# Taking the constant 160 off again on VectorE instead of ScalarE, in a fused layer kernel on eight cores

## What is computed

```python
xn    = layernorm(x)                              # per token, no weights
B, C  = xn @ W2 + b2, xn @ W3 + b3                # 16 columns each
delta = softplus(xn @ W1 + b1)                    # 1024 columns
s     = xn * delta * sum(B * C, axis=-1)          # the einsums collapse to this
xh    = xn @ H                                    # Hadamard, 1024 x 1024, / 32
sc    = max(abs(xh)) / 7                          # per token
xq    = clip(round(xh / sc), -8, 7) * sc
wq    = ternary(weight)                           # -1, 0, 1 times a scale per output row
g     = silu(xq @ wq.T)
out   = x + s * g
```

## Time and profile before

| | us |
|---|---|
| median of 3 runs | 528.99 (528.32 to 529.50) |
| the profiled execution | 529.43 |
| its span on the slowest core, core 0 | 527.9 |
| spans of the eight cores | 523.0 to 527.9 |

### The profile page before, as it was taken

The page is one execution under the profiler, slowest core; times in us unless marked ns, Lnnn a source line. Parts: engine busy times, 40 slices in busy tenths (PEclk is TensorE's granted clock), DMA queues, the critical chain, the costliest instruction groups (busy, mean ns, idle before and its releaser), DMA issues.

```text
span 527.9 us, 7192 instructions; the slowest of 8 cores (523.0 to 527.9 us)
## 1 busy us (share of the span) xinstructions
PE 351.1 (67%) x1696; PEld 149.1 (28%) x1696; DVE 305.9 (58%) x600; ACT 344.0 (65%) x393; POOL 323.4 (61%) x215
## 2 busy tenths in 40 slices
PE   0023260997979697877978787787789779757200
PEld 0001220443424243332433333333333334322000
DVE  1418886455766666666667666667666654542210
ACT  1603143569796979888888888888888777654220
POOL 6000160112677777777777777777777777767763
PEclk9997575798979899997989899989988999896655
DMA  7992321243654454444445445444544334222110
GB/s 146 247 261 65 110 61 23 57 94 78 140 120 116 120 153 122 120 122 120 119 120 121 120 125 128 124 125 119 133 135 133 80 81 99 61 61 60 41 78 40
DMA packets 80973, 57.78 MB, mean 109 GB/s; under 512 B 70435, under 2 KB 70564, under 8 KB 80932
## 3 DMA queue, kind: packets, MB, share of 16 engines
q1 hardware_dynamic: 72916, 34.19, 29.9%
q0 software_dynamic: 8016, 23.14, 13.6%
HBM read 25.93 MB, written 16.78 MB: 81 GB/s over the span
## 4 chain that ended last, share of the span: by engine, by line
POOL 48%; DVE 17%; issue 12%; PE 9%; DMA 5%; ACT 4%; POOLq 1%; DVEq 1%; SPq 1%; ACTq 0%
POOL ob L33 13%; POOL t4b L33 13%; POOL t1b L33 11%; DVE t3b L33 7%; POOL uT L33 5%; POOL vT L33 5%; DMA xnT<-xnb 3%; DVE tbf L33 3%; DMA xb<-x 3%; DVE absum L33 2%; PE psZ L268 1%; PE psZ L269 1%; PE psO L289 1%; DVE cst L33 1%; PE psO L290 1%
## 5 line engine op out<-in xcount | busy, mean ns | idle before, releaser
L33 POOL TENSOR_TENSOR t4b<-t3b,o3s 128x1024 f32<-128x1024 f32 x32 | 75.2, 2351 | 69.4 <-DVE t3b L33 69.4
L289 PE MATMUL psO<-ternT,xqT 128*128 128x512 bf16 x256 | 100.6, 393 | 13.6 <-DMA xqT<-xqb 8.3
L268 PE MATMUL psZ<-W1c,xnT 128*128 128x512 bf16 x256 | 101.0, 395 | 0.5 <-DVE bcw L33 0.5
L269 PE MATMUL psZ<-W1c,xnT 128*128 128x512 bf16 x256 | 100.3, 392 | 0.0
L290 PE MATMUL psO<-ternT,xqT 128*128 128x512 bf16 x256 | 100.2, 391 | 0.0
L312 PE MATMUL psXH<-Hs,uT 128*128 128x512 bf16 x128 | 58.3, 456 | 45.2 <-ACT xqm L33 41.0
L33 DVE SCALAR_TENSOR_TENSOR t3b<-xnb,cc,t1b 128x1024 f32<-128x1024 bf16 x32 | 41.1, 1284 | 73.4 <-POOL t1b L33 73.0
L33 POOL TENSOR_TENSOR ob<-xb,t4b 128x1024 f32<-128x1024 f32 x32 | 75.4, 2355 | 4.6
L33 POOL TENSOR_TENSOR t1b<-del,s 128x1024 f32<-128x1024 bf16 x32 | 68.6, 2143 | 7.9 <-ACT s L33 4.1
L33 ACT ACTIVATE esb<-psO,nsa 128x1024 f32<-128x1024 f32 x32 | 35.7, 1114 | 52.1 <-DVE o3s L33 51.6
L33 POOL TENSOR_TENSOR uT<-xnT 128x512 bf16<-128x512 bf16 x32 | 37.2, 1164 | 38.3 <-DMA xnT<-xnb 37.4
(11 more groups left out here) (53 smaller groups left out, 509.3 us busy)
## 6 DMA issues: line engine op xcount, KB each, us to landing
xb<-x SPq DMA_DIRECT2D x32, 512.0 KB, 4.1
out<-ob POOLq DMA_DIRECT2D x32, 512.0 KB, 3.4
wfst<-wf POOLq DMA_DIRECT2D x8, 512.0 KB, 4.2
W1c<-w POOLq DMA_DIRECT2D x8, 256.0 KB, 17.6
Hs<-hpk SPq DMA_DIRECT2D x1, 512.0 KB
xnT<-xnb SPq DMA_TRANSPOSE x32, 3.0
xqT<-xqb SPq DMA_TRANSPOSE x32, 3.1
W23s<-w POOLq DMA_DIRECT2D x1, 64.0 KB, 3.5
```

The costliest lines, as they stand in the source:

```text
L33: inst = fn(*a, **kw)
L268: pe.matmul(psZ1[:, 0:512], lh, W1c[ic][:, 0:512], start=(ic == 0), stop=False)
L269: pe.matmul(psZ1[:, 512:1024], lh, W1c[ic][:, 512:1024], start=(ic == 0), stop=False)
L289: pe.matmul(ps[:, 0:512], lh, ternT[:, ic * DM:ic * DM + 512], start=(ic == 0), stop=(ic == KC - 1))
```

## The change

The instruction that makes `xqb` goes from ScalarE to VectorE. There it is a `tensor_single_scalar` with the immediate -160.0 and `ALU.add`, bfloat16 in and out, written between `dot` and `o3s`. The wait for the transpose of the tile before goes with it, and VectorE gets a wait on `sRND`, which ScalarE sets when `xqm` is done. The semaphore `sXQB` that SP waits for is now set by VectorE.

```diff
@@ scalar
                     ac.wait_ge(sMX, u + 1)
                     ac.activation(xqm[:], psXH[:], AF.Identity, scale=inv[u % 2][:],
                                   bias=c160s[:], _inc=(sRND, u + 1))
-                    if u >= 1:
-                        ac.wait_ge(sTXQa[(u - 1) % 2], 16 * ((u - 1) // 2 + 1))
-                    ac.activation(xqbf[:], xqm[:], AF.Identity, bias=nc160s[:], _inc=(sXQB, u + 1))
                 w_ = c - 3
@@ vector
                     dv.tensor_reduce(dot[td % 2][:], prod[:], AX.X, ALU.add)
+                uq = c - 1
+                if 0 <= uq < nt:
+                    dv.wait_ge(sRND, uq + 1)
+                    if uq >= 1:
+                        dv.wait_ge(sTXQa[(uq - 1) % 2], 16 * ((uq - 1) // 2 + 1))
+                    dv.tensor_single_scalar(xqbf[:], xqm[:], -160.0, ALU.add, _inc=(sXQB, uq + 1))
 
                 w_ = c - 3
```

## The result

| | before | after |
|---|---|---|
| median of 8 runs, us | 529.10 (528.32 to 529.76) | 567.02 (566.31 to 568.78) |
| ratio after / before | | 1.0722 [1.0706, 1.0737] |
| the profiled execution, us | 529.43 | 566.57 |
| spans of the eight cores, us | 523.0 to 527.9 | 560.2 to 565.0 |

The change costs 38 us. The forecast was 560.8 with a range to 565.5, so the direction and the size of the main term held, and the time lies 6.2 us over the forecast and 1.5 over the range.

A forecast was written before the change was run, and what follows sets the result against it. POOL's own instructions plus `t3b` were taken to set the 12.72 us pass. 31.4 us from the start through held passes 5 to 27, plus 0.4 at the end, took the span from 527.9 to 559.7; median 560.8, range 531 to 565.5.

The forecast's parts named there:

- The two chains of a pass: From the start of `o3s`: POOL reaches the next `t1b` in 11.66 us, ACT's chain reaches `xqb` in 11.69, 0.03 later.
- The hold: `xqb` starting during a POOL instruction is held, ending 0.28 us after it (0.2 to 0.45); alone it takes 0.45.
- The held pass: With `xqb` held through `t1b`, a pass takes 14.19 us against 12.72, or 1.47 more, and the state keeps itself.
- Where it starts: `o3s` of pass 4 at 128.6, `t1b` of pass 5 at 140.3; held passes 5 to 27, `t1b` of pass 28 31.4 later.
- Where it ends: In pass 28 `dumpa`'s ACT slot is gone, `xqb` starts within `vT`, and the normal pass returns.
- have 2.6 us and cost nothing more: In held passes, `bcw`, `prod`, `dot` and a late `psZ` fit under the wait for `xqb`: no added cost.
- the drain has slack: After the full passes, the drain was said to have slack; only 0.4 us was added for the end.
- The rest of the allowance: In passes 28 to 30 a held `xqb` may delay the next POOL instruction by 0.2 us each.
- The race is won: Rival: `xqb` starts just ahead of `t1b` and stays early; 0.14 to 0.45 us more a pass, 531 to 542; chance 0.22.
- No meeting with POOL: Rival: bfloat16 `xqb` is not held by POOL, takes 0.45 us, POOL sets the pass; 527 to 529; chance 0.09.
- More: Rival: held passes in which something else also slips, over 566 us; chance 0.04.

The follow-up runs named there:

- Run 4: Kernel before plus an independent instruction of `xqb`'s form (the dummy) on VectorE between `dot` and `o3s`: 556.41 us against 530.21, ratio 1.0445.
- run 9: Changed kernel with `xqb` made at the same place by a reduction over single elements, offset 160 left out: 548.61 us against 530.46, ratio 1.0329.
- prod_psum: Changed kernel with `prod` reading one factor from PSUM instead of both from SBUF: 563.83 us against 530.18, ratio 1.0636.
- run 1: Changed kernel with `xqm` ahead of `del` on ScalarE: 546.93 us against 530.21, ratio 1.0314.
- run 7: Changed kernel with `xqm` ahead of `del` on ScalarE and `prod` reading one factor from PSUM: 532.16 us against 530.18, ratio 1.0039.
- run 5: Kernel before plus an independent instruction of `xqb`'s form between `dot` and `o3s`, and `prod` with one factor from PSUM: 532.25 us against 530.46, ratio 1.0024.
- dummy_prod: The same as run 5: kernel before plus the independent instruction, with `prod` reading one factor from PSUM: 532.25 us against 530.46.
- pool_prod: Kernel before with `t1b` ahead of `uT` and `vT` on POOL and `prod` with one factor from PSUM: 514.85 us against 530.46, ratio 0.9698.

## Why the prediction held, and where it failed

**The two chains of a pass.** Right. POOL's chain was put at 11.66 us from `o3s` to the next `t1b`; the rows of after give 423.88 - 412.22 = 11.66. ACT's chain was put at 11.69 to the start of `xqb`; in the passes before it is 11.75 (`t1b` 0.10 ahead of `xqb`, not 0.03). The link from the end of `xqm` to DVE is 0.24 us (409.80 - 409.56) and not the 0.17 that I had from the earlier trace rows. The error was 0.07 against a margin of 0.03, and it went the safe way: the prediction said that one more wait in the queue could only add. Had it been as much shorter, the race would have been won.

**The hold.** Right in kind and size. `xqb` ends 0.28 us after POOL's instruction, as taken from `cst`; alone it takes 0.43 us, within the 0.4 to 0.5. The 0.28 was half of the 0.55 of `cst`, on the ground of half the element time; the rows give 0.753 against 0.486, which is 1.5 to 1, so that it came out to 0.01 us has luck in it. Run 4 shows it without any dependence, run 9 shows its absence in another form of instruction. The held pass was put at 14.19 and is 14.17.

**Where it starts.** Right: on core 1 `o3s` of pass 4 at 128.62 (128.6 said), `t1b` of pass 5 at 140.28 (140.3 said), `t1b` of pass 28 at 466.35 (466.7 said). That it fits to 0.02 us is partly luck, since `t1b` of pass 5 lies between 139.15 and 141.76 on the eight cores. So 31.1 of the 38 us are the term that the prediction worked out. (They are 0.65 from the start and 21 passes at 1.45 us, since passes 5 and 7 of core 0 already took 14.17 and 14.20 us before.)

**Where it ends.** Here a step failed, and it took the time out of the range: the one that says of `bcw`, `prod`, `dot` and a late `psZ` that they "have 2.6 us and cost nothing more", with "in pass 28 ... the normal pass returns". From `t1b` of pass 28 to the end there were 527.9 - 435.25 = 92.65 us before and 565.0 - 466.35 = 98.65 after: 6.0 more, where 0.4 was said. It is made of three passes of 14.17, 14.16 and 11.67 where there were 12.71, 12.69 and 10.08 (4.5 us), and of one in the drain, 11.55 instead of 10.07 (1.5). Pass 28 on core 1, DVE and POOL:

```profile
465.73 0.50 DVE L33 TENSOR_TENSOR prod<-bcw 128x16 f32<-128x16 f32 x1
...
466.61 2.16 DVE L33 TENSOR_SCALAR xqb<-xqm 128x1024 bf16<-128x1024 bf16 x1
...
465.06 1.15 POOL L33 TENSOR_TENSOR vT<-xnT 128x512 bf16<-128x512 bf16 x1
466.35 2.14 POOL L33 TENSOR_TENSOR t1b<-del,s 128x1024 f32<-128x1024 bf16 x1
```

and on core 3, the core that did what was predicted:

```profile
465.22 0.93 DVE L33 TENSOR_TENSOR prod<-bcw 128x16 f32<-128x16 f32 x1
...
466.69 0.99 DVE L33 TENSOR_SCALAR xqb<-xqm 128x1024 bf16<-128x1024 bf16 x1 [0.27 <-ACT xqm L33]
...
464.94 1.16 POOL L33 TENSOR_TENSOR uT<-xnT 128x512 bf16<-128x512 bf16 x1
466.25 1.15 POOL L33 TENSOR_TENSOR vT<-xnT 128x512 bf16<-128x512 bf16 x1
467.54 2.14 POOL L33 TENSOR_TENSOR t1b<-del,s 128x1024 f32<-128x1024 bf16 x1
```

On both, `xqm` was ready early, as the prediction had it: 13.1 us after the last `t1b` (452.20 and 453.38). On core 3 `prod` was caught by `uT`, was free at 466.15, and `xqb` went in during `vT`. On core 1 `prod` came 1.69 us later in its pass, was caught by `vT`, was free only at its end, and `xqb` met `t1b`. What came late is TensorE. The first matmul of `psO` and the one that ends the columns for `bcw`, core 1 and then core 3:

```profile
459.65 0.38 PE L289 MATMUL psO<-ternT,xqT 128*128 128x512 bf16 x1 [1.45 <-ACT s L33]
...
464.79 0.35 PE L303 MATMUL psZ<-W23s,xnT 128*128 128x32 bf16 x8
```

```profile
460.83 0.38 PE L289 MATMUL psO<-ternT,xqT 128*128 128x512 bf16 x1 [1.46 <-ACT s L33]
...
464.28 0.36 PE L303 MATMUL psZ<-W23s,xnT 128*128 128x32 bf16 x8
```

Both start 7.45 us after `t1b`. Then core 1 needs 5.14 us and core 3 3.45. The granted clock in just these stretches (window us, its length, us, busy us and instructions of PE, PEld, DVE, ACT, POOL, PEclk, DMA share, GB/s), core 1 and then core 3:

```profile
459.60:465.30 5.70, 5.61 (x25) 2.33 (x25) 2.42 (x4) 4.93 (x6) 4.83 (x5) 0.70 0.40 108
```

```profile
460.80:464.80 4.00, 3.92 (x25) 1.89 (x25) 2.41 (x4) 3.35 (x5) 3.30 (x3) 1.00 0.16 34
```

Core 3 had the full 2.4 GHz for all of it; core 1 spent part of it at 1.2 GHz. Both had waited 1.45 us for `s` just before, so that wait alone does not tell why only one clock fell, and it stays open. So the step "a late `psZ` costs nothing more" counted the delay as if it could only add to a wait, and missed that a delay of `prod` moves `xqb` into the next instruction of POOL. As long as `xqm` is the last to arrive, a late `prod` is free (in pass 26 on core 1 it was held for 0.52 us and the pass was 14.16). In pass 28 `xqm` is early, and `prod` decides. The other cores agree: seven of the eight have a granted clock of 0.70 in this stretch, `prod` 0.62 us ahead of `t1b`, held to the end of `vT`, and three more held passes; core 3 alone leaves. The program has eight cores, and one that stays is enough for the longer time.

Two things are needed there, then, a late `bcw` and the hold of `prod`. `prod_psum` takes away the second, but does not separate them: in it TensorE had a clock of 1.00 in this stretch on all eight cores (3.92 to 3.94 us of work, as on core 3 here), for a reason that is not known, and on seven `bcw` started 2.6 us ahead of `t1b`. Only its core 6 has a late one (1.23 ahead); there the free `prod` let `xqb` in during `vT`, and the pass was 12.70. Pass 14 in runs 1 and 7 separates them on eight cores. For a `bcw` as late as in pass 28 (0.92 to 0.95 ahead) runs 4 and 5 do: with `prod` held the dummy starts 0.27 us after `t1b` and the pass is 14.16 to 14.19 (14.5 in pass 10), with `prod` free it starts 0.11 to 0.12 ahead and the pass is 12.88 to 12.90 (pass 7 of cores 2, 3, 5 and 6 of `dummy_prod`, rows in the last section).

**The long pass in the drain.** The 1.5 us of pass 32 are of another kind. They appear on cores 1 and 6 only, which with core 5 have the longest spans. Core 1, POOL and then DVE:

```profile
512.90 2.35 POOL L33 TENSOR_TENSOR ob<-xb,t4b 128x1024 f32<-128x1024 f32 x1
...
512.97 2.29 DVE L33 TENSOR_TENSOR cc<-dot,sa 128x1 f32<-128x1 f32 x1
```

`cc` is one column with two SBUF inputs. It started 0.07 us after `ob` and was held to its end; on core 0 it started at 512.27, 0.18 ahead of `ob`, and took 0.16. `xqm` waited for it (515.41 against 512.59 on core 0), so `xqb` started 0.44 us after `t1b` and was held in it. So the sentence "the drain has slack" failed too: a third small instruction, `cc`, can push `xqb` into the long hold. It was late because its `psXH` was, on a TensorE that had worked at 1.2 GHz until about 507.6.

**The size of the miss.** The span was put at 559.7. Core 3 has 560.2. The slowest, core 1, has 565.0: 5.6 from the end (4.5 and 1.5, less the 0.4 allowed), less 0.35 from the start. Outside the span there are 1.6 us, as said, and the median is 0.45 us above the profiled execution and not 0.44 below. The rest of the allowance, 0.2 for each pass 28 to 30 even in the normal state, was not needed: on core 3 `t1b` started 0.14 us after `vT`, as always.

**The rivals.** *The race is won* did not happen in any of passes 5 to 27 on any of the eight cores. Its mechanism exists (run 1, core 6), but for the steady state, with `xqb` held in `vT`, at another price than the 0.14 to 0.45 us a pass that I gave: none, 12.70 us a pass. At that price this rival would have lain near 530 us (an estimate), a little under the lower end of the range. A pass in which `xqb` starts just ahead of `t1b` does cost something, 0.18 to 0.24 us (last section), so the 0.4 given for it was too much. *No meeting with POOL* is refuted for this form by run 4 and shown for a reduction by run 9. The Trainium skill (SBUF — State Buffer, "Who interferes with whom") sorts the two forms in the same way. *More*, "held passes in which something else also slips", had 0.04; it is what happened, by 1 us, and should have had more, since the profile before already shows `prod` held in most of its passes, and in passes 5 and 7 of core 0 by `t1b`, at 14.2 us.

## What to carry to other kernels

An instruction that moves to an engine that shares something with another one costs by when it starts, not by how long it is: write down, for each candidate place, which instruction of the neighbour runs at that moment and when that ends. Look at each short instruction ahead of it in the same queue too, since a hold of 16 columns, or of one, can push the large one into the next and longer hold. And where a state keeps itself from pass to pass, ask what could carry each of the eight cores out of it, since one that stays sets the time.

## What the runs showed of the hardware

- **One operand in PSUM frees a two-input instruction.** `prod` with both factors in SBUF took 0.17 to 2.1 us, by what POOL did; with one factor from PSUM 0.170 to 0.174 us in all 32 instances on each of the eight cores of five kernels.
- **The hold works in both directions, less POOL's start.** In `pool_prod`, core 6, `t3b` was held by `uT` until 238.72 and then ran for 1.09 us, and the `vT` behind it became longer:

```profile
237.57 1.15 POOL L33 TENSOR_TENSOR uT<-xnT 128x512 bf16<-128x512 bf16 x1
...
238.87 1.95 POOL L33 TENSOR_TENSOR vT<-xnT 128x512 bf16<-128x512 bf16 x1
...
237.68 2.13 DVE L33 SCALAR_TENSOR_TENSOR t3b<-xnb,cc,t1b 128x1024 f32<-128x1024 bf16 x1 [0.44 <-POOL t1b L33]
```

  `vT` ends at 240.82, 1.01 us after `t3b` (239.81), where it takes 1.15 alone. So the first 0.14 us of a POOL instruction go on beside DVE. A held `xqb` ends just 0.28 us after POOL's instruction, which is 0.14 after the start of the next: it costs POOL nothing, and that is why the won race was free. Where `xqb` or the dummy starts just ahead of `t1b`, POOL's instruction grows by the overlap less this 0.14. `dummy_prod`, core 5, pass 7, where the two overlap for 0.31 us and `t1b` takes 2.30 instead of 2.13:

```profile
170.20 0.43 DVE L33 TENSOR_SCALAR cst<-W1c 128x1024 bf16<-128x1024 bf16 x1
...
170.32 2.30 POOL L33 TENSOR_TENSOR t1b<-del,s 128x1024 f32<-128x1024 bf16 x1
```

- **Just ahead is not always ahead.** The prediction read from the earlier trace rows that a DVE instruction which starts just before one of POOL's is not held. Before `vT` and `t1b` this is so. Before `uT`, which follows the issue of a store on POOL, it is not: in the kernel before, core 7, `prod` started at 429.93 and `uT` at 430.14, and `prod` took 1.41 us, to the end of `uT`.
- **Part of a held instruction is done during the hold.** `xqb` takes 0.43 us alone and ends 0.28 after the release.
- **Small clock differences become large.** 1.7 us of TensorE time, at a granted clock of 0.70 instead of 1.00, on an engine that had slack, decided between spans of 560 and 562 to 565 us.
